# Banded attention scored per half block of queries, in plain fp32 on 32x64 tiles

## The chip, the cores and the metric

The kernel runs on one core of a Trainium2 chip. The metric is the device time of one execution in microseconds. The median of three runs of the kernel before is 2627.7 us (2626.91 to 2631.21).

## The reference, cut to what matters

8192 tokens of width 512 are layer-normalised; to the input are added a banded attention and a feed-forward. The attention has 16 heads of 32. Blocks are of 128 tokens, and a query sees the keys at a distance of at most 128:

```python
qkv = (xn @ Wqkv + bqkv).reshape(B, S, 3, H, Dh)
kwin = concat(previous block, own block, next block)      # 384 keys
scores = einsum('bhnqd,bhnkd->bhnqk', qb, kwin) / sqrt(512)
mask = (abs(kpos - qpos) <= 128) & (kpos >= 0) & (kpos < S)
attn = softmax(where(mask, scores, -1e30))
out = einsum('bhnqk,bhnkd->bhnqd', attn, vwin) ; out @ Wout + bout
x + attention(xn) + feed_forward(xn)
```

## The kernel before, in words

The program has three stages: it prepares the feed-forward's weights, runs the feed-forward over all tokens and leaves its result (`partial`) and the transposed, normalised tokens in DRAM, and then runs `attention_stage`, from about 1130 us to the end. Only this last stage is changed.

It goes over 32 tiles `i` of two blocks (256 tokens) and, in each, over 4 groups `c` of four heads: 128 steps `t`, `i, c = where(t)`. The order on every engine is written out by hand as a loop over `t`, with semaphores between the engines. The letters used below: `b` is one of the tile's two blocks, `h` one of the group's four heads, `u = 4b + h`.

On TensorE (PE) one step is, in this order:

- `scores(t, 0)` (L1176): for the four heads, each on its own 32-row tile of the array and in its own PSUM bank, 128 queries by 384 keys. Queries and keys are kept as a high and a low part in the fast reduced format (`q_hi`, `q_lo`, `k_hi`, `k_lo`, type F32R), so that three passes (high x high, low x high, high x low) make up one product: 12 matmuls.
- four turns of `turn_probs(t-1, 1, part)` (L1193), three 128x128 transposes of one head's probabilities by a matmul with the identity, and `run_a(t, part)` (L1105), six of the 24 matmuls that project queries and keys for step `t + 2`.
- `scores(t, 1)`.
- `probs_times_values(t-1)` (L1217): plain fp32, the four heads on four 32-column tiles of the array. Two key blocks are seen by both query blocks (256 columns), two by one of them (128 columns): 16 matmuls, all into one bank.
- four turns of `turn_probs(t, 0, part)` and `run_b(t, part)`: three of the 12 matmuls of a V projection (L1114) or of the output projection (L1123).

VectorE (DVE) finds each row's maximum with the mask added while it copies the scores out of PSUM (`find_max`, L1006), takes reciprocals (L1017), normalises three heads of four (L1021), and writes the low parts `q_lo`, `k_lo` (`qk_low`, L1034, L1038) and `oT_lo` (L1027). ScalarE (ACT) does the exponentials (`exp`, L928), copies the transposed probabilities out of PSUM (`copy_pT`, L938), and writes `q_hi`, `k_hi` (`qk_high`, L954, L957), `oT_hi` (L946) and the values (`take_v`, L921). GpSimd (POOL) normalises the fourth head (L888), copies the last two key blocks of a tile to the front of the ring in every second tile (`copy_keys`) and adds the output's bias. SyncE (SP) holds the DMA queue: tokens in, `partial` in, `out` out.

`values` is a ring of 6 blocks, `oT_hi` and `oT_lo` hold two tiles (8 slots). PE waits for a block of V by `v_done`.

Of the kernel before, what the change touches and what calls it, by code (L numbers as in the profile page):

```python
# [22 lines left out]
P = 128  # L23
# [638 lines left out]
def attention_stage(nc, loaded, xT_dram, partial, out):  # L662
# [6 lines left out]
    VR = 6  # L669
    XR = 3  # L670

    ctx = ExitStack()
    with ctx:
# [14 lines left out]
        mask = sb("mask", [P, 3 * P], F32)  # L688
# [13 lines left out]
        oT_hi = sb("oT_hi", [P, 2, DC, T], F32R)  # L702
        oT_lo = sb("oT_lo", [P, 2, DC, T], F32R)
# [13 lines left out]
        k0_hi, k0_done = sem("k0_hi"), sem("k0_done")  # L717
        qk_hi_done, qk_done = sem("qk_hi_done"), sem("qk_done")
        keys_copied = sem("keys_copied")
        v_done = sem("v_done")  # L720
        scored = sem("scored")
# [40 lines left out]
        def window(i, b):  # L762
            first, last = max(2 * i - 1 + b, 0), min(2 * i + 1 + b, NBLK - 1)
            base = 2 * i - 1 + b
            return slice((first - base) * P, (last - base + 1) * P)

        def blocks_seen(i, b):

            return range(0 if 2 * i - 1 + b >= 0 else 1, 3 if 2 * i + 1 + b < NBLK else 2)
# [22 lines left out]
        def job_release(n):  # L792

            t, k = divmod(n, 3)
            if k == 0:
                return (qk_done, job_a(t) + 1) if job_a(t) is not None else None
            if k == 1:
                return (oT_done, t) if 1 <= t <= STEPS else None
            b = job_b(t)
            if b is None:  # L800
                return None
            return (v_done, 2 * b[1] + b[2] + 2) if b[0] == "v" else (out_added, 2 * b[1] + b[2] + 1)

        def wait_job_bank(pe, n):
# [6 lines left out]
            elif n % 2 == 0:  # L811
                pe.wait_ge(v_done, 2)
            else:
                pe.wait_ge(qk_done, 2)
# [17 lines left out]
        def _(sp):  # L832
# [18 lines left out]

            for j in range(-1, XR - 1):
                load_x(j)
            sp.wait_ge(wout_lo_done, 1)
            for b in range(2):
                load_part(0, b)
            for i in range(NT + 1):
                if 1 <= i:
# [4 lines left out]
                if i + XR - 1 < NT:  # L863
                    load_x(i + XR - 1)
            for b in range(2):
# [3 lines left out]
        def _(pool):  # L869
            identity_on_pool(pool, nc, ident, zeroed, ident_done)  # L870
            nc.gpsimd.memset(mask[:, :], 0.0).then_inc(zeroed, 1)
            pool.wait_ge(zeroed, 2)
            nc.gpsimd.affine_select(out=mask[:, 0:P], in_=mask[:, 0:P], compare_op=ALU.is_ge, fill=NEG,
                                    base=0, pattern=[[1, P]], channel_multiplier=-1).then_inc(mask_done, 1)
            nc.gpsimd.affine_select(out=mask[:, 2 * P:3 * P], in_=mask[:, 2 * P:3 * P], compare_op=ALU.is_ge,
                                    fill=NEG, base=0, pattern=[[-1, P]], channel_multiplier=1).then_inc(mask_done, 1)
# [6 lines left out]
            def normalise_last_head(t, b):  # L883
                i, _ = where(t)
                cols = window(i, b)
                u = b * HC + HC - 1
                pool.wait_ge(rcp_done, 2 * (2 * t + b) + 2)
                nc.gpsimd.tensor_scalar(probs[:, u, cols], probs[:, u, cols], sum_rcp[:, u:u + 1], None, ALU.mult  # L888
                                        ).then_inc(last_head_normalised, 1)

            def copy_keys(u):
                i, c = where(u)
                pool.wait_ge(qk_done, u + 1)
                nc.gpsimd.tensor_copy(k_hi[:, c, 0:2, :], k_hi[:, c, 4:6, :])
                nc.gpsimd.tensor_copy(k_lo[:, c, 0:2, :], k_lo[:, c, 4:6, :]).then_inc(keys_copied, 1)
# [20 lines left out]
        def _(act):  # L916
            def take_v(i, r, number, bank):
                act.wait_ge(job_filled, number)
                if i >= 2:
                    act.wait_ge(pv_done, 4 * i - 4)  # L920
                nc.scalar.copy(values[:, (2 * i + 1 + r) % VR, :], job_ps[:, bank, :]).then_inc(v_done, 1)  # L921

            def exp(t, b, h):
                i, _ = where(t)
                cols = window(i, b)
                u = b * HC + h
                act.wait_ge(maxed, 8 * t + u + 1)
                nc.scalar.activation(probs[:, u, cols], probs[:, u, cols], ACT.Exp, bias=neg_max[:, u:u + 1], scale=-1.0,  # L928
                                     accum_out=prob_sum[:, u:u + 1]).then_inc(exped, 1)

            def copy_pT(t, b, h):
                i, _ = where(t)
                seen = blocks_seen(i, b)
                first = 3 * at(i, b)
# [3 lines left out]
                nc.scalar.copy(pT[:, h, first + seen.start:first + seen.stop, :].rearrange("p w t -> p (w t)"),  # L938
                               pT_ps[:, h % 2, seen.start * P:seen.stop * P]).then_inc(pT_done, 1)

            def oT_high(t):
                i, c = where(t)
                act.wait_ge(pv_done, t + 1)
                if i >= 2 and c == 0:
                    act.wait_ge(job_filled, B_NUMBER[4 * (i - 1) + 2])
                nc.scalar.copy(oT_hi[:, i % 2, c, :], job_ps[:, pv_bank(t), 0:T]).then_inc(oT_hi_done, 1)  # L946

            def qk_high(u, number, bank):
# [3 lines left out]
                if u >= DC:  # L952
                    act.wait_ge(scored, 2 * (u - DC) + 2)
                nc.scalar.activation(q_hi[:, c, :, :].rearrange("p b t -> p (b t)"), job_ps[:, bank, 0:T], ACT.Identity,  # L954
                                     bias=qk_bias[:, c:c + 1], scale=1.0)
                half = new_keys_at(i)
                nc.scalar.activation(k_hi[:, c, half:half + 2, :].rearrange("p b t -> p (b t)"),  # L957
                                     job_ps[:, bank, T:2 * T], ACT.Identity,
                                     bias=qk_bias[:, DC + c:DC + c + 1], scale=1.0).then_inc(qk_hi_done, 1)
# [393 lines left out]
```

## Time and profile before

| | us |
|---|---|
| median of the runs | 2627.7 |
| profiled execution, its own time | 2629.41 |
| its span, first to last instruction | 2627.6 |
| PE busy | 2576.2 (98%) |
| ACT busy | 1638.1 (62%) |
| DVE busy | 1592.0 (61%) |
| POOL busy | 631.8 (24%) |
| mean granted clock of PE | 0.989 |

PE's matmuls are pipelined, so a record's duration is longer than the time between two starts; what a matmul costs in a stream is read from the starts. PEld is the load of the stationary operand, which lies beside the matmul before. A plain fp32 matmul leaves two load records and two matmul records. In a form such as "128*32 128x256" the first pair is rows and columns of the stationary operand, the second the moving one.

### The profile page before, as it was taken

To read this page: it belongs to the slowest core of one execution; us is meant where nothing else is said; L and a number is where in the kernel's file an instruction comes from. 1 tells how busy PE (TensorE), PEld (TensorE's weight loads), DVE (VectorE), ACT (ScalarE), POOL (GpSimd) and SP (SyncE) were. 2 spreads that over 40 slices of the span, in tenths; PEclk is the share of its full clock that TensorE was granted. 3 is DMA by queue.
4 is the path that set the end of the run, shared out by engine and by line. 5 is a ranking of instruction groups with operands and counts; after the bars stand their busy time and mean duration, and the time that the engine had idled before them with its cause. 6 is when DMAs were issued, how large, how long until landed. Compare 5 with 4: busy or idle time off the path is not lost.

```text
span 2627.6 us, 55989 instructions
## 1 busy us (share of the span) xinstructions
PE 2576.2 (98%) x19728; PEld 2090.2 (80%) x19728; DVE 1592.0 (61%) x4779; ACT 1638.1 (62%) x4260; POOL 631.8 (24%) x595
## 2 busy tenths in 40 slices
PE   6999999999999999989999999999999999999998
PEld 4888888888888888868888888888888888888885
DVE  5444444444444444357777777777777777777775
ACT  6333333333333333358888888888888888888886
POOL 0011111111111111033333333333333333333332
PEclk7999999999999999999999999999999999999999
DMA  5422222222222222021121111112111111112110
GB/s 181 146 80 81 80 80 80 80 80 80 80 80 80 80 80 64 33 81 34 34 65 34 53 46 42 58 41 58 34 61 39 42 58 42 58 34 65 34 46 29
DMA packets 188361, 167.43 MB, mean 64 GB/s; under 512 B 11328, under 2 KB 143424, under 8 KB 187632
## 3 DMA queue, kind: packets, MB, share of 16 engines
q1 hardware_dynamic: 188000, 164.41, 20.2%
q8 instruction: 132, 2.16, 0.4%
q14 instruction: 85, 0.70, 0.1%
q0 software_dynamic: 144, 0.17, 0.0%
HBM read 97.43 MB, written 67.11 MB: 63 GB/s over the span
## 4 chain that ended last, share of the span: by engine, by line
PE 55%; ACT 1%; issue 0%; DVE 0%; POOL 0%; POOLq 0%; ACTq 0%
PE pT_ps L1193 14%; PE job_ps L1105 14%; PE score_ps L1176 7%; PE job_ps L1123 7%; PE job_ps L1217 7%; PE job_ps L1114 7%; ACT wqkv_raw L928 1%; ACT wqkv_raw L938 0%; PE job_ps L1237 0%; PE score_ps L1227 0%; DVE wqkv_raw L1006 0%; DVE k_lo L1038 0%; ACT q_hi L954 0%; ACT k_hi L957 0%; POOL wout_raw L899 0%
## 5 line engine op out<-in xcount | busy, mean ns | idle before, releaser
L928 ACT ACTIVATE wqkv_raw<-wqkv_raw,neg_max 128x384 f32<-128x384 f32 (+1 forms) x1024 | 633.3, 619 | 186.3 <-DVE neg_max L1006 181.5
L888 POOL TENSOR_SCALAR wqkv_raw<-wqkv_raw,sum_rcp 128x384 f32<-128x384 f32 (+1 forms) x256 | 372.9, 1457 | 960.1 <-DVE sum_rcp L1017 960.1
L494 ACT ACTIVATE relu<-up_ps,fc_scale 128x512 f32<-128x512 f32 x256 | 176.2, 688 | 656.2 <-PE up_ps L625 656.2
L938 ACT COPY wqkv_raw<-pT_ps 128x384 f32<-128x384 f32 (+1 forms) x1024 | 484.7, 474 | 74.4 <-PE pT_ps L1193 74.1
L1193 PE MATMUL pT_ps<-ident,wqkv_raw 128*128 128x128 f32 x3040 | 513.4, 277 | 8.1 <-ACT wqkv_raw L938 7.7
L1006 DVE CUSTOM_DVE_ANT_0 wqkv_raw<-score_ps,mask 128x384 f32<-128x384 f32 (+1 forms) x1024 | 503.5, 548 | 5.7 <-PE score_ps L1176 1.6
L568 DVE SCALAR_TENSOR_TENSOR sq<-up_ps,relu 128x512 f32<-128x512 f32 x256 | 177.0, 692 | 531.8 <-ACT relu L494 530.4
L1193 PEld LDWEIGHTS pT_ps<-ident,wqkv_raw 128*128 128x128 f32 x3040 | 360.0, 140 | 119.1 <-ACT wqkv_raw L938 42.6
L635 PE MATMUL down_ps<-proj_T,sq_hi 128*128 128x512 f32 x1024 | 408.9, 399 | 0.9 <-DVE sq_lo L551 0.9
L637 PE MATMUL down_ps<-proj_T,sq_lo 128*128 128x512 f32 x1024 | 404.3, 395 | 0.0
L621 PE MATMUL up_ps<-f_xT_hi,fc_T 128*128 128x512 f32 x1024 | 399.2, 390 | 1.4 <-DVE low L539 1.4
L623 PE MATMUL up_ps<-f_xT_lo,fc_T 128*128 128x512 f32 x1024 | 399.2, 390 | 0.0
L1105 PE MATMUL job_ps<-xT_hi,wqkv_hi 128*128 128x256 f32 x1024 | 329.0, 321 | 0.1
L1021 DVE TENSOR_SCALAR wqkv_raw<-wqkv_raw,sum_rcp 128x384 f32<-128x384 f32 (+1 forms) x768 | 298.2, 416 | 17.9
L1017 DVE RECIPROCAL sum_rcp<-prob_sum 128x2 f32<-128x2 f32 x512 | 85.0, 166 | 354.5 <-ACT wqkv_raw L928 354.0
L1105 PE MATMUL job_ps<-xT_hi,wqkv_lo 128*128 128x256 f32 x1024 | 287.9, 281 | 0.0
L1105 PE MATMUL job_ps<-xT_lo,wqkv_hi 128*128 128x256 f32 x1024 | 287.8, 281 | 0.0
L454 POOL TENSOR_TENSOR f_y<-f_y,part_in 128x512 f32<-128x512 f32 x64 | 86.9, 1389 | 665.1 <-DVE f_y L559 665.1
L635 PEld LDWEIGHTS down_ps<-proj_T,sq_hi 128*128 128x128 f32 x1024 | 193.4, 189 | 43.9 <-DVE sq_lo L551 2.2
L621 PEld LDWEIGHTS up_ps<-f_xT_hi,fc_T 128*128 128x128 f32 x1024 | 192.3, 188 | 44.0 <-DVE low L539 2.2
L637 PEld LDWEIGHTS down_ps<-proj_T,sq_lo 128*128 128x128 f32 x1024 | 193.0, 188 | 43.0
L623 PEld LDWEIGHTS up_ps<-f_xT_lo,fc_T 128*128 128x128 f32 x1024 | 192.3, 188 | 42.5
(126 smaller groups left out, 4228.2 us busy)
## 6 DMA issues: line engine op xcount, KB each, us to landing
xT_hi<-xT SPq DMA_DIRECT2D x65, 256.0 KB, 3.8
xT_lo<-xT SPq DMA_DIRECT2D x65, 256.0 KB, 4.5
f_x_in<-in_L_attn_x SPq DMA_DIRECT2D x64, 256.0 KB, 3.2
xT<-f_xT_hi SPq DMA_DIRECT2D x64, 256.0 KB, 2.6
xT<-f_xT_lo SPq DMA_DIRECT2D x64, 256.0 KB, 2.8
part_in<-in_L_attn_x SPq DMA_DIRECT2D x64, 256.0 KB, 3.4
partial<-f_y SPq DMA_DIRECT2D x64, 256.0 KB, 2.0
wout_raw<-partial SPq DMA_DIRECT2D x64, 256.0 KB, 2.8
```

Of the source, the lines that this page charges most:

```text
L621: nc.tensor.matmul(up_ps[:, s % 2, :], fc_T[:, k, cols], xT_hi[:, par, k, :], start=(k == 0), stop=False)
L623: nc.tensor.matmul(up_ps[:, s % 2, :], fc_T[:, k, cols], xT_lo[:, par, k, :], start=False, stop=False)
L635: nc.tensor.matmul(down_ps[:, b, :], sq_hi[:, s % 2, t], proj_T[:, s, :], start=(s == 0), stop=False)
L637: last = nc.tensor.matmul(down_ps[:, b, :], sq_lo[:, s % 2, t], proj_T[:, s, :], start=False, stop=(s == FB - 1))
L888: nc.gpsimd.tensor_scalar(probs[:, u, cols], probs[:, u, cols], sum_rcp[:, u:u + 1], None, ALU.mult).then_inc(last_head_normalised, 1)
L928: nc.scalar.activation(probs[:, u, cols], probs[:, u, cols], ACT.Exp, bias=neg_max[:, u:u + 1], scale=-1.0, accum_out=prob_sum[:, u:u + 1] ...
L938: nc.scalar.copy(pT[:, h, first + seen.start:first + seen.stop, :].rearrange("p w t -> p (w t)"), pT_ps[:, h % 2, seen.start * P:seen.stop ...
L1006: nc.vector.tensor_tensor_reduce(out=probs[:, u, cols], in0=score_ps[:, h, cols], in1=mask[:, cols], scale=-SCORE_SCALE, scalar=3e38, op0= ...
L1021: nc.vector.tensor_scalar(probs[:, u, cols], probs[:, u, cols], sum_rcp[:, u:u + 1], None, ALU.mult).then_inc(normalised, 1)
L1105: last = nc.tensor.matmul(job_ps[:, bank, is_k * T:(is_k + 1) * T], w[:, k, col:col + P], tokens, start=(m == 0), stop=(m == PASSES * DC - 1))
L1114: last = nc.tensor.matmul(job_ps[:, bank, :], a[:, k, x_slot(i) + r, :], w[:, k, 2 * D:3 * D], start=(n == 0), stop=(n == PASSES * DC - 1))
L1193: last = nc.tensor.transpose(pT_ps[:, h % 2, w * P:(w + 1) * P], probs[:, u, w * P:(w + 1) * P], ident[:, :])
```

## The change

Each block of 128 queries is treated as two halves `s` of 64. A half sees 64 queries by 320 keys instead of 384: `KEYS = 320`, and in column `j` of half `s` stands the key `64 s + j` of the old window.

- Scores: queries and keys are kept once, as plain F32 (`queries`, `keys`). Head `h` and half `s` go to the 32x64 tile at row `32 h` and column `64 s`: 8 plain fp32 matmuls of 320 columns instead of 12 of 384. The copies of low parts (`qk_low`) are gone; ACT writes the queries (`take_q`), DVE the keys (`take_k`).
- The mask has 320 columns; at the two ends of the sequence the keys that don't exist are filled by a memset and the maximum is taken for each half apart.
- Transposes: an even head is transposed from column 0 in two pieces, an odd head from column 64 in two pieces, and the 64 columns left over by an even head (256 to 319) and by the odd head after it (0 to 63), which lie side by side in `probs`, in one more: five for two heads instead of six.
- Values: since the two halves' windows begin 64 keys apart, and odd heads are cut 64 keys further on than even ones, V is kept twice, in `values` and, shifted by 64 tokens, in `half_on`. The second copy is made by two DMAs per block on SP (`move_values`), and PE waits for them by `v_moved`. For each half there is a part of 2 x 64 columns, two of 64, and two of 64 on 64x32 tiles (64 keys only; even heads in rows 0 to 63, odd heads in rows 64 to 127): 40 matmuls instead of 16.
- `values` has a ring of 5, `oT_hi` and `oT_lo` one of 6 slots.

```diff
-    VR = 6
+    VR = 5
     XR = 3
+    HALF = P // 2
+    KEYS = 2 * P + HALF
+    OR = 6
+    FAR = -NEG * SCORE_SCALE
...
-        q_hi = sb("q_hi", [P, DC, 2, P], F32R)
-        q_lo = sb("q_lo", [P, DC, 2, P], F32R)
-        k_hi = sb("k_hi", [P, DC, 6, P], F32R)
-        k_lo = sb("k_lo", [P, DC, 6, P], F32R)
+        queries = sb("queries", [P, DC, 2, P], F32)
+        keys = sb("keys", [P, DC, 6, P], F32)
         values = sb("values", [P, VR, D], F32)
-        probs = wqkv_raw[:, 0:2, :].rearrange("p a (u k) -> p (a u) k", k=3 * P)
+        half_on = sb("values_half_on", [P, VR, D], F32)
+        probs = wqkv_raw.rearrange("p a n -> p (a n)")[:, 0:2 * HC * KEYS].rearrange("p (u k) -> p u k", k=KEYS)
...
+            def move_values(m):
+
+                sp.wait_ge(v_done, m + 1)
+                if m >= VR:
+                    sp.wait_ge(pv_done, 4 * ((m - VR + 1) // 2) + 4)
+                sp.dma_start(half_on[HALF:P, (m - 1) % VR, :], values[0:HALF, m % VR, :]).then_inc(v_moved, 16)
+                sp.dma_start(half_on[0:HALF, m % VR, :], values[HALF:P, m % VR, :]).then_inc(v_moved, 16)
...
+                if 2 * i + 2 < NBLK:
+                    move_values(2 * i + 2)
...
+                if 2 * i + 3 < NBLK:
+                    move_values(2 * i + 3)
...
-                if i >= 2:
-                    act.wait_ge(pv_done, 4 * i - 4)
+                m = 2 * i + 1 + r
+                if m >= VR:
+                    act.wait_ge(pv_done, 4 * ((m - VR + 1) // 2) + 4)
+                    act.wait_ge(v_moved, 32 * (m - VR + 1))
...
-                if i >= 2 and c == 0:
-                    act.wait_ge(job_filled, B_NUMBER[4 * (i - 1) + 2])
-                nc.scalar.copy(oT_hi[:, i % 2, c, :], job_ps[:, pv_bank(t), 0:T]).then_inc(oT_hi_done, 1)
-
-            def qk_high(u, number, bank):
+                if i >= 1 and c == OR - DC:
+                    act.wait_ge(job_filled, B_NUMBER[4 * i + 2])
+                nc.scalar.copy(oT_hi[:, t % OR, :], job_ps[:, pv_bank(t), 0:T]).then_inc(oT_hi_done, 1)
...
-            def qk_low(u, bank):
+                nc.vector.tensor_tensor(oT_lo[:, t % OR, :], job_ps[:, pv_bank(t), 0:T],
+                                        oT_hi[:, t % OR, :].bitcast(F32), ALU.subtract).then_inc(oT_done, 1)
+
+            def take_k(u, bank):
                 i, c = where(u)
                 half = new_keys_at(i)
-                dve.wait_ge(qk_hi_done, u + 1)
-                nc.vector.scalar_tensor_tensor(q_lo[:, c, :, :].rearrange("p b t -> p (b t)"), job_ps[:, bank, 0:T],
-                                               qk_bias[:, c:c + 1],
-                                               q_hi[:, c, :, :].rearrange("p b t -> p (b t)").bitcast(F32),
-                                               ALU.add, ALU.subtract)
-                nc.vector.scalar_tensor_tensor(k_lo[:, c, half:half + 2, :].rearrange("p b t -> p (b t)"),
-                                               job_ps[:, bank, T:2 * T], qk_bias[:, DC + c:DC + c + 1],
-                                               k_hi[:, c, half:half + 2, :].rearrange("p b t -> p (b t)").bitcast(F32),
-                                               ALU.add, ALU.subtract).then_inc(qk_done, 1)
+                dve.wait_ge(q_done, u + 1)
+                nc.vector.tensor_scalar(keys[:, c, half:half + 2, :].rearrange("p b t -> p (b t)"),
+                                        job_ps[:, bank, T:2 * T], qk_bias[:, DC + c:DC + c + 1], None, ALU.add
+                                        ).then_inc(k_done, 1)
...
-                for pass_ in range(PASSES):
-                    q = q_lo if pass_ == 1 else q_hi
-                    keys = k_lo if pass_ == 2 else k_hi
-                    for h in range(HC):
-                        rows = slice(h * DH, (h + 1) * DH)
-                        last = nc.tensor.matmul(score_ps[:, h, cols], q[rows, c, place, :],
-                                                keys[rows, c, first + seen.start:first + seen.stop, :],
-                                                start=(pass_ == 0), stop=(pass_ == PASSES - 1),
-                                                tile_position=(h * DH, 0))
+                for h in range(HC):
+                    rows = slice(h * DH, (h + 1) * DH)
+                    window = keys[rows, c, :, :].rearrange("p a t -> p (a t)")
+                    for s in range(2):
+                        start = (keys_start(i) + b) * P + s * HALF
+                        first, last_ = first_key(i, b, s), last_key(i, b, s)
+                        last = nc.tensor.matmul(score_ps[half_rows(s), h, first:last_],
+                                                queries[rows, c, at(i, b), half_rows(s)],
+                                                window[:, start + first:start + last_],
+                                                start=True, stop=True, tile_position=(h * DH, s * HALF))
...
-                for w in blocks_seen(i, b):
-                    last = nc.tensor.transpose(pT_ps[:, h % 2, w * P:(w + 1) * P], probs[:, u, w * P:(w + 1) * P],
+                for w in range(2):
+                    start = w * P + h % 2 * HALF
+                    last = nc.tensor.transpose(pT_ps[:, h % 2, w * P:(w + 1) * P], probs[:, u, start:start + P],
                                                ident[:, :])
+                if h % 2:
+                    both = probs[:, u - 1:u + 1, :].rearrange("p u k -> p (u k)")[:, 2 * P:3 * P]
+                    last = nc.tensor.transpose(pT_ps[:, 1, 2 * P:3 * P], both, ident[:, :])
...
-                    pe.wait_ge(v_done, min(2 * i + 3, NBLK))
+                    pe.wait_ge(v_moved, 32 * min(2 * i + 3, NBLK))
                 pe.wait_ge(pT_done, 8 * t + 2 * HC)
-                parts = []
-                for blk in (2 * i, 2 * i + 1):
-                    first, second = (3 * place + blk - (2 * i - 1 + at(i, place)) for place in range(2))
-                    parts.append((blk, slice(0, 2), slice(first, second + 1, second - first)))
-                for b, blk in enumerate((2 * i - 1, 2 * i + 2)):
-                    if 0 <= blk < NBLK:
-                        place = at(i, b)
-                        seen = 3 * place + 2 * b
-                        parts.append((blk, slice(place, place + 1), slice(seen, seen + 1)))
-                for n, (blk, places, seen) in enumerate(parts):
-                    for h in range(HC):
-                        head = c * HC + h
-                        strip = slice(h * DH, (h + 1) * DH)
-                        last = nc.tensor.matmul(job_ps[strip, bank, places.start * P:places.stop * P],
-                                                values[:, blk % VR, head * DH:(head + 1) * DH], pT[:, h, seen, :],
-                                                start=(n == 0), stop=(n == len(parts) - 1), tile_position=(0, h * DH))
+                for s in range(2):
+                    for part in range(5):
+                        for h in range(HC):
+                            head = c * HC + h
+                            strip = slice(h * DH, (h + 1) * DH)
+                            odd = h % 2
+                            v = half_on if s != odd else values
+                            base = 2 * i - 1 + (s if odd else 0)
+                            rows, row = slice(0, P), 0
+                            if part == 0:
+                                blk, places = base + 1, slice(0, 2)
+                                first, second = (3 * place + 1 - at(i, place) for place in range(2))
+                                seen = slice(first, second + 1, second - first)
+                            elif part < 3:
+                                b = part - 1
+                                blk, place = base + 2 * b, at(i, b)
+                                places, seen = slice(place, place + 1), slice(3 * place + b, 3 * place + b + 1)
+                                if blk < 0 and not odd and s == 0:
+                                    continue
+                            else:
+                                b = part - 3 if odd else 4 - part
+                                if 2 * i + b == (0 if odd else NBLK - 1):
+                                    continue
+                                place, rows, row = at(i, b), half_rows(odd), odd * HALF
+                                blk = base + b + (-1 if odd else 2)
+                                places, seen = slice(place, place + 1), slice(3 * place + 2, 3 * place + 3)
+                            out_ = job_ps[strip, bank, 0:T].rearrange("p (a t) -> p a t", t=P)[:, places, half_rows(s)]
+                            last = nc.tensor.matmul(out_, v[rows, blk % VR, head * DH:(head + 1) * DH],
+                                                    pT[rows, h | 1 if part > 2 else h, seen, half_rows(s)],
+                                                    start=(part == 0), stop=(part == 4), tile_position=(row, h * DH))
```

On PE, from the last scores of a step over the values to the first transposes, where the tile's newest block of V is waited for (`score_ps` scores, `job_ps<-wqkv_raw` probabilities times values, `pT_ps` transposes), before:

```order
L1176 MATMUL score_ps<-k_hi,q_hi 128x384 [waits maxed]
L1176 MATMUL score_ps<-k_hi,q_hi 128x384 x3
L1176 MATMUL score_ps<-k_hi,q_lo 128x384 x4
L1176 MATMUL score_ps<-k_lo,q_hi 128x384 x4
L1217 MATMUL job_ps<-wqkv_raw,values 32x256 [waits pT_done,v_done]
L1217 MATMUL job_ps<-wqkv_raw,values 32x256 x7
L1217 MATMUL job_ps<-wqkv_raw,values 32x128 x8
L1193 MATMUL pT_ps<-ident,wqkv_raw 128x128 [waits normalised,pT_done]
```

and with the change (line numbers of the changed kernel):

```order
L1191 MATMUL score_ps<-keys,queries 64x320 [waits maxed]
L1191 MATMUL score_ps<-keys,queries 64x320 x7
L1249 MATMUL job_ps<-wqkv_raw,values 32x2x64 [waits pT_done,v_moved,v_done]
L1249 MATMUL job_ps<-wqkv_raw,values_half_on 32x2x64
L1249 MATMUL job_ps<-wqkv_raw,values 32x2x64
L1249 MATMUL job_ps<-wqkv_raw,values_half_on 32x2x64
L1249 MATMUL job_ps<-wqkv_raw,values 32x64
L1249 MATMUL job_ps<-wqkv_raw,values_half_on 32x64
```

Sixteen matmuls of 64 columns follow the four of 2 x 64, by turns on `values` and `half_on`, the last eight of them on 64x32 tiles; then the same 20 once more for the other half. The order around them has not moved.

On PE, the start of a step after the first scores, before, a head's transposes ahead of six projections:

```order
L1193 MATMUL pT_ps<-ident,wqkv_raw 128x128 [waits normalised,pT_done]
L1193 MATMUL pT_ps<-ident,wqkv_raw 128x128 x2
L1105 MATMUL job_ps<-xT_hi,wqkv_hi 128x256
L1105 MATMUL job_ps<-xT_lo,wqkv_hi 128x256
L1105 MATMUL job_ps<-xT_hi,wqkv_lo 128x256
```

and with the change, two heads:

```order
L1208 MATMUL pT_ps<-ident,wqkv_raw 128x128 [waits normalised,pT_done]
L1208 MATMUL pT_ps<-ident,wqkv_raw 128x128
L1123 MATMUL job_ps<-xT_hi,wqkv_hi 128x256 [waits oT_done]
L1123 MATMUL job_ps<-xT_lo,wqkv_hi 128x256
L1123 MATMUL job_ps<-xT_hi,wqkv_lo 128x256
L1123 MATMUL job_ps<-xT_hi,wqkv_hi 128x256
L1123 MATMUL job_ps<-xT_lo,wqkv_hi 128x256
L1123 MATMUL job_ps<-xT_hi,wqkv_lo 128x256
L1208 MATMUL pT_ps<-ident,wqkv_raw 128x128 [waits normalised,pT_done]
L1208 MATMUL pT_ps<-ident,wqkv_raw 128x128
L1212 MATMUL pT_ps<-ident,wqkv_raw 128x128
```

An even head has two transposes, an odd one three.

On SP's queue, one tile in the steady part, with the change:

```order
L866 DMA values_half_on<-values 64x512 [waits pv_done,v_done]
L867 DMA values_half_on<-values 64x512
L859 DMA out<-wout_raw 128x512 [waits y_done]
L855 DMA wout_raw<-partial 128x512 [waits out_added]
L859 DMA out<-wout_raw 128x512 [waits y_done]
L855 DMA wout_raw<-partial 128x512 [waits out_added]
L849 DMA xT_hi<-xT 128x4x128 [waits job_filled]
L849 DMA xT_hi<-xT 128x4x128
L849 DMA xT_lo<-xT 128x4x128 x2
L866 DMA values_half_on<-values 64x512 [waits pv_done,v_done]
```

The moves (L866, L867) are new, ahead of the two stores and behind the loads of tokens; the rest stands as before.

## Rows read from the trace of the kernel before

**Rows 1.** The page, busy us, share of the span and instructions of each engine.
```profile
PE 2576.2 (98%) x19728; PEld 2090.2 (80%) x19728; DVE 1592.0 (61%) x4779; ACT 1638.1 (62%) x4260; POOL 631.8 (24%) x595
```
**Rows 2.** Stretch of the steady steps: us, busy (x) by engine, PEclk, DMA share, GB/s.
```profile
1378.37:2522.73 1144.36, 1144.36 (x11601) 933.04 (x11600) 837.68 (x2950) 941.09 (x2752) 391.78 (x350) 1.00 0.16 48
```
**Rows 3.** Waits, 1500 to 2500 us: who <- whom: us, times, longest.
```profile
POOL wqkv_raw L888 <- DVE sum_rcp L1017: 657.7, 175, 4.6
DVE sum_rcp L1017 <- ACT wqkv_raw L928: 243.4, 350, 1.1
ACT wqkv_raw L928 <- DVE neg_max L1006: 124.7, 88, 1.4
...
PEld score_ps L1176 <- issue: 32.0, 88, 0.4
```
**Rows 4.** Chain, 1801.7 to 1813.3 us: start, us up to the next piece, what.
```profile
1801.84 0.73 PE score_ps L1176 x9
1802.57 0.48 PE pT_ps L1193 x3
1803.05 0.71 PE job_ps L1105 x6
1803.76 0.33 PE pT_ps L1193 x3
...
1807.59 1.44 PE job_ps L1217 x32
...
1809.51 0.70 PE job_ps L1123 x3
```
**Rows 5.** Timeline of PE, narrow windows in one values part: first start, us, matmuls overlapping.
```profile
1807.53 0.42 PE L1217 MATMUL job_ps<-wqkv_raw,values 128*32 128x256 f32 x4
1807.77 0.61 PE L1217 MATMUL job_ps<-wqkv_raw,values 128*32 128x256 f32 x8
1808.20 0.51 PE L1217 MATMUL job_ps<-wqkv_raw,values 128*32 128x256 f32 x8
1808.41 0.51 PE L1217 MATMUL job_ps<-wqkv_raw,values 128*32 128x128 f32 x12
1808.63 0.40 PE L1217 MATMUL job_ps<-wqkv_raw,values 128*32 128x128 f32 x8
1808.96 0.55 PE L1193 MATMUL pT_ps<-ident,wqkv_raw 128*128 128x128 f32 x3
```
**Rows 6.** Line L1217, 1807.5 to 1808.3: ns min/median/max, first and last start.
```profile
L1217 PE MATMUL job_ps<-wqkv_raw,values x16: 379/379/404, 1807.5 to 1808.2; 128*32 128x256 f32 x16
```
**Rows 7.** Timeline of PE, 1806.7 to 1807.4 us, the three score passes.
```profile
1806.80 0.45 PE L1176 MATMUL score_ps<-k_hi,q_hi 32*128 32x384 f32 x4
1807.09 0.34 PE L1176 MATMUL score_ps<-k_hi,q_lo 32*128 32x384 f32 x4
1807.26 0.34 PE L1176 MATMUL score_ps<-k_lo,q_hi 32*128 32x384 f32 x4
```
**Rows 8.** ACT's timeline, and line L1217 on PE: V's copy and its reader.
```profile
1435.95 0.61 ACT L921 COPY values<-job_ps 128x512 f32<-128x512 f32 x1
...
L1217 PE MATMUL job_ps<-wqkv_raw,values x32: 272/326/404, 1441.3 to 1442.6; 128*32 128x256 f32 x16, 128*32 128x128 f32 x16
```
**Rows 9.** The page, DMA issues on SP: KB each, median us to landing.
```profile
xT_lo<-xT SPq DMA_DIRECT2D x65, 256.0 KB, 4.5
...
partial<-f_y SPq DMA_DIRECT2D x64, 256.0 KB, 2.0
```
**Rows 10.** Chain while the pipeline fills, 1130 to 1170 us.
```profile
1158.42 0.37 ACT k_hi L957
1158.81 0.48 DVE q_lo L1034
```
**Rows 11.** The tail: its chain, and its stretch (columns as in rows 2).
```profile
2611.45 2.40 PE job_ps L1217 x24
...
2600.00:2628.00 28.00, 17.83 (x120) 11.58 (x112) 8.55 (x31) 9.09 (x30) 6.67 (x6) 0.80 0.11 39
```

More of the change, by code:

```diff
@@ L760, in new_keys_at, with half_rows, first_key, last_key @@
             return keys_start(i) + 2
[L762 to L769, printed above, removed]
+        def half_rows(s):
+            return slice(s * HALF, (s + 1) * HALF)
+        def first_key(i, b, s):
+            return max(0, -((2 * i - 1 + b) * P + s * HALF))
+        def last_key(i, b, s):
+            return min(KEYS, (NBLK - (2 * i - 1 + b)) * P - s * HALF)
+        def at_edge(i, b):
+            return 2 * i + b == 0 or 2 * i + b == NBLK - 1
         def job_a(t):
@@ L937, in copy_pT @@
                     act.wait_ge(pv_done, t)
-                nc.scalar.copy(pT[:, h, first + seen.start:first + seen.stop, :].rearrange("p w t -> p (w t)"),
-                               pT_ps[:, h % 2, seen.start * P:seen.stop * P]).then_inc(pT_done, 1)
+                nc.scalar.copy(pT[:, h, first:first + count, :].rearrange("p w t -> p (w t)"),
+                               pT_ps[:, h % 2, 0:count * P]).then_inc(pT_done, 1)
             def oT_high(t):
@@ L953, in qk_high @@
                     act.wait_ge(scored, 2 * (u - DC) + 2)
[L954 to L959, printed above, removed]
+                nc.scalar.activation(queries[:, c, :, :].rearrange("p b t -> p (b t)"), job_ps[:, bank, 0:T],
+                                     ACT.Identity, bias=qk_bias[:, c:c + 1], scale=1.0).then_inc(q_done, 1)
             act.wait_ge(wqkv_here, 64)
@@ L1005, in find_max @@
                     u = b * HC + h
[L1006 to L1008 removed]
+                    if not at_edge(i, b):
+                        nc.vector.tensor_tensor_reduce(out=probs[:, u, :], in0=score_ps[:, h, 0:KEYS], in1=mask[:, :],
+                                                       scale=-SCORE_SCALE, scalar=3e38, op0=ALU.add, op1=ALU.min,
+                                                       accum_out=neg_max[:, u:u + 1]).then_inc(maxed, 1)
+                        continue
+                    for s in range(2):
+                        rows, first, last = half_rows(s), first_key(i, b, s), last_key(i, b, s)
+                        outside = slice(0, first) if first else slice(last, KEYS)
+                        nc.vector.memset(probs[rows, u, outside], FAR)
+                        done = nc.vector.tensor_tensor_reduce(out=probs[rows, u, first:last],
+                                                              in0=score_ps[rows, h, first:last], in1=mask[rows, first:last],
+                                                              scale=-SCORE_SCALE, scalar=3e38, op0=ALU.add, op1=ALU.min,
+                                                              accum_out=neg_max[rows, u:u + 1])
+                    done.then_inc(maxed, 1)
             def normalise(t, b):
[L1011 to L1012 removed]
                 for pair in range(2):
@@ L1059, in _ @@
             nc.vector.tensor_tensor(out_bias[:, :], score_ps[:, 0, :], bout_wide[:, :], ALU.add).then_inc(bias_added, 1)
-            dve.wait_ge(mask_done, 2)
-            dve.wait_ge(k0_hi, 1)
-            for c in range(DC):
-                last = nc.vector.scalar_tensor_tensor(k_lo[:, c, keys_start(0) + 1, :], job_ps[:, 0, c * P:(c + 1) * P],
-                                                      qk_bias[:, DC + c:DC + c + 1],
-                                                      k_hi[:, c, keys_start(0) + 1, :].bitcast(F32), ALU.add, ALU.subtract)
-            last.then_inc(k0_done, 1)
+            dve.wait_ge(mask_done, 4)
             for u in range(2):
-                qk_low(u, u)
+                take_k(u, u)
             for t in range(STEPS + 3):
@@ L1122, in project_out @@
                     a = oT_lo if o_low else oT_hi
-                    last = nc.tensor.matmul(job_ps[:, bank, :], a[:, i % 2, k, at(i, b) * P:(at(i, b) + 1) * P],
+                    last = nc.tensor.matmul(job_ps[:, bank, :], a[:, (DC * i + k) % OR, at(i, b) * P:(at(i, b) + 1) * P],
                                             w[:, k, :], start=(n == 0), stop=(n == PASSES * DC - 1))
```

80 lines of the change are left out of this document (37 added, 43 removed).

## The prediction

> **What bounds the kernel now.** I read the page's shares first, then the stretches, the waits, the chain and last the single matmul starts. PE is busy 98% of the span [rows 1]. The change touches only the attention stage, the last 1,500 us. Its steady part is the stretch from 1378.37 to 2522.73 us, 100 steps (11,601 matmul records, 116 to a step). PE is busy in all of the 1144.36 us, ACT 941 (82%), DVE 838 (73%), POOL 392 (34%), at clock 1.00, the 2.4 GHz level [rows 2]. One step is therefore 11.44 us of PE, and no other engine fills it. The waits agree: in 1,000 us POOL waits for DVE, DVE for ACT and ACT for DVE; for PE's matmuls there is no line at all, and its weight loads have lines of at most 32 us, once a step, which lie beside a matmul that still runs [rows 3]. The chain gives the step piece by piece, each up to the next piece's start [rows 4]: scores 0.73, twice; transposes three at a time, 0.33, or 0.48 right after scores or values; six projections 0.71; values 1.44; three output (or V) projections 0.70. With four turns each for the two projections that adds up to 11.5. So only PE's time counts, and each piece must be repriced.
>
> **Prices from single starts.** In the values part four matmuls, one per 32-column tile, start together. Groups of 256 columns start 0.215 us apart (1807.77 to 1808.20 is two groups), groups of 128 columns 0.11 [rows 5]. Each plain fp32 matmul leaves two records, so 256 columns cost 2 x 0.215: time goes with columns. Four groups of each make 1.30 of the 1.44; 0.14 is left. It splits as follows: the last group (0.11 after 1808.63, so 1808.74) is followed by the transposes at 1808.96, 0.22 instead of 0.11, so 0.11 for changing the tiling; and the longest of them took 404 ns where the median is 379, 0.025 for a weight load that nothing covers [rows 6]. In the scores a pass of four matmuls of 384 columns costs 0.17, the first one 0.29 [rows 7]; 0.73 less three passes leaves 0.22 for entering, leaving and an uncovered load of 128 columns.
>
> **The change part by part, per step.**
> Transposes: 20 instead of 24, each 0.33/3 = 0.11 [rows 4]: **-0.44**. In the runs of two after a change of tiling the extra 0.15 (0.48 against 0.33) stays.
> Scores: 8 plain fp32 matmuls of 320 columns in 8 tiles replace 12 of 384 in 4 tiles. If all 8 run side by side, two records of 0.215 x 320/256 = 0.27 take the place of three passes of 0.17: 0.54 for 0.51. Around them 0.22 stays, or 0.17 if the uncovered load of 64 columns is half of that of 128 (0.29 - 0.17 = 0.12). That is +0.03 or -0.02 each, two a step: between +0.06 and -0.04. I take **0**, from the middle, since the load is smaller but twice as many matmuls must start.
> Values: 40 matmuls for 16. Each query half has one part of 2 x 64 columns and four of 64, two records each: together 4 groups of 128 columns and 16 of 64. The first are 4 x 0.11 = 0.44. The second are not in the trace; by columns they are 0.055 each, 0.88. Together 1.32 for 1.30: +0.02. Columns streamed are the same; the parts are only cut finer.
> Changes of tiling inside the values: the last two parts of each half have 64 rows, so the tiles go 128x32, 64x32, 128x32, 64x32: three changes where none was. No row shows a change of the row height alone. Lower bound 0 (the columns of the tiles stay), upper bound 0.22 (all that surrounds the scores). The nearest row is the exit from the values themselves, 0.11 and 0.025 for the load: I take 0.14. Three of them: **+0.42**, between 0 and +0.66.
> Sum: -0.44 + 0 + 0.02 + 0.42 = **0.00 us a step**.
>
> **Off PE, costed at nothing.** Subtracting and writing q_lo and k_lo goes, k is written once by DVE; every exp, maximum and normalisation has 320 columns, every second copy of transposes 256. All this relieves ACT, DVE and POOL, which have 200 us and more of cover in the steady part [rows 2]; if PE became faster by 0.4 us a step they would still not be reached. At the two ends of the sequence the maximum is split in two and a fill is added, in 8 of 128 steps, under the same cover. The ring for the output's operands shrinks from 8 slots to 6: ACT's copy at every fourth step now waits for an output projection that PE ends half a step earlier. Nothing queues behind it.
> New is the move of V: two DMAs of 128 KB per block on SP's queue, and PE's first values matmul of each four steps waits for them. The copy of V ends at 1435.95 + 0.61 = 1436.56 and PE starts on that block at 1441.3 [rows 8], so 4.7 us of cover. No row shows a copy within SBUF; transfers of twice its size on the same queue land after 2.0 to 4.5 us [rows 9]. SP reaches the move in time: what stands ahead waits for events of the step before, and the stores queued behind it wait for output projections that come later. Price 0; if the slower end and the second DMA's place in the queue add up to 5.7 us, 1 us x 32 blocks = 32 us.
> Outside the steady part the other engines are on the path. While the pipeline fills, the chain holds k_hi and q_lo, 0.37 + 0.48 [rows 10], and the same two a second time later; both go: -0.85 x 2. In the tail some ten exps and copies on the chain lose a sixth of about 0.5 us, -0.8, against three more changes of tiling in the last values, which take 2.40 at a mean clock of 0.80 in that stretch [rows 11]: +0.4. Together -2.
>
> So the profiled execution, 2629.4, becomes 2627.4. The median of the runs lies 1.7 below it, which gives **2625 us**, no change: 0.2% of 2627.7 is 5.3 us, what a measurement of this kernel can tell. It is 0.04 us a step, less than my prices are good for: the forecast's own spread of +-0.12 a step is 2610 to 2640.
>
> **Rivals.**
> A, the change of tiling is nearly free, since the column tiles stay and only the row height changes. Then 0.42 falls away: -54, **2571**. For it: the values keep their four 32-column tiles throughout. Against: the exit from the values costs its 0.11 and the surroundings of the scores 0.22, so no change of tiling in the trace is free.
> B, on the other side: **groups of 64 columns do not get below 0.11**, because four loads and four starts per group need it. In the trace the densest stretch is four matmuls per 0.11 us, 27 ns each [rows 5]; the change asks for 14 ns each. 16 groups x 0.055 = +0.88 a step, +113, **2738**; from 0.059 us per group on the change is slower by over 0.2%. Against it: the first four matmuls span 0.42 us together where the longest takes 0.404, so they start within 20 ns [rows 5, 6], and the time of a group halves exactly with its columns from 256 to 128, as a stream does and a start does not. The Trainium skill (TensorE: Matmul & The Clock Gate, section "Wait — 56ns, not 53.3ns?") has a floor of about 25 ns from start to start however small the matmul; by it a group costs 0.10 and the time would be about 2717. The trace neither reaches below it in the mean (27 ns) nor keeps to it inside a group.
> C, the 64-row parts take turns: even heads sit in rows 0 to 63, odd ones in rows 64 to 127, and both write one PSUM bank. That doubles 8 groups of 0.055: +0.44, +56, **2681**. The Trainium skill (TensorEngine Tiling (Array Packing), section "Gotcha 1: PSUM Pressure") says that different row tiles cannot access the same bank at the same time. In the trace the four row tiles of the scores each have their own bank and the four column tiles of the values share one, so neither speaks for or against; their output partitions differ, as those of the column tiles do.
> D, the change does not do what it says: the two column halves of a row tile take turns in the scores, which then cost 4 x 0.27. +0.54 x 2 = 1.08 a step, +138, **2763**. The trace has four row tiles side by side and four column tiles side by side, not both at once.
> E, V's move is late: +32, about 2657.
>
> **How the numbers follow.** Forecast 50% (18 faster, 17 same, 15 slower), A 16, B and its milder forms, groups between 0.06 and 0.11, 13, C 9, D 7, E and others 5. Faster 0.18 + 0.16 + 0.01 = 0.35; same 0.18; slower 0.47. The range takes in A and, upwards, C, E and B with groups of up to 0.10 (16 x 0.045 x 128 = 92 us): 2570 to 2720. It leaves out D and the full B, about 14%.
>
> **What would show it.** Right: in steady state a period of 11.44 us; transposes 0.22 and 0.33 by turns; scores near 0.73, with two groups of eight starts 0.27 apart; values near 1.9 us with gaps of 0.2 at three places; no PE wait for V's move. A shows as values of 1.5; B as small groups 0.11 apart; C as parts three and four alone at 0.11; D as scores of 1.3; E as PE idle before the values of every fourth step. A period off by more than 0.12 us makes the forecast wrong.

## The result, and the profile after

The changed kernel takes 2646.36 us (median of 4 runs, 2645.09 to 2647.46), the kernel before beside it 2629.45. The ratio is 1.0065, with an interval from 1.0047 to 1.0082: slower by 0.65%, where no change was forecast. Run once more beside the experiments it gave 2647.11 us and a ratio of 1.0068 (1.0054 to 1.0081). The profiled execution has a span of 2645.7 us against 2627.6, 18.1 us more.

The steady steps came out as priced. The chain of waits of the changed kernel in one of them (start, us up to the next piece, what), which answers to [rows 4]:

```profile
1813.41 0.72 PE score_ps L1191 x16
1814.14 1.87 PE job_ps L1249 x80
1816.01 0.37 PE pT_ps L1208 x2
1816.38 0.70 PE job_ps L1141 x3
1817.08 0.22 PE pT_ps L1208 x2
1817.30 0.11 PE pT_ps L1212
```

The scores take 0.72 us, as before (0.73). The values take 1.87 instead of 1.44. The transposes take 0.22 and 0.33 by turns, 0.37 right after a change of tiling. The stretch that answers to [rows 2] is again filled by PE, while the other engines are relieved (columns as there):

```profile
1378.37:2522.73 1144.36, 1144.36 (x16795) 901.59 (x16780) 733.88 (x2850) 871.07 (x2649) 337.02 (x299) 1.00 0.21 60
```

16,795 matmul records at 168 a step are 100 steps in 1144.36 us, as before. Read from the first scores of steps 4 and 124, the period is 11.453 us against 11.442. Over the steady part that is 1.3 us, so 17 of the 18 lie elsewhere. The first scores of single steps, read from PE's timeline, show where:

| us | before | changed | difference |
|---|---|---|---|
| first scores of step 0 | 1154.0 | 1155.7 | +1.7 |
| step 0 to step 4 | 41.4 | 45.8 | +4.4 |
| step 4 to step 124 | 1373.1 | 1374.4 | +1.3 |
| step 124 to the end | 59.1 | 69.8 | +10.7 |

The pipeline fills in steps 0 to 3 and drains in steps 124 to 127, and these are the steps with the blocks at the edge of the sequence. There the changed kernel's DVE does this for one head (timeline: start us, us; line 1034 is the fill, 1035 the maximum):

```profile
1157.63 0.17 DVE L1034 MEMSET wqkv_raw<- 64x128 f32 x1
1157.81 0.35 DVE L1035 CUSTOM_DVE_ANT_0 wqkv_raw<-score_ps,mask 64x192 f32<-64x192 f32 x1
1158.09 0.08 DVE L1035 DVE_READ_ACCUMULATOR2_ANT neg_max<- 64x1 f32 x1
1158.22 0.11 DVE L1034 MEMSET wqkv_raw<- 64x64 f32 x1
1158.34 0.43 DVE L1035 CUSTOM_DVE_ANT_0 wqkv_raw<-score_ps,mask 64x256 f32<-64x256 f32 x1
1158.70 0.08 DVE L1035 DVE_READ_ACCUMULATOR2_ANT neg_max<- 64x1 f32 x1
1158.86 0.17 DVE L1034 MEMSET wqkv_raw<- 64x128 f32 x1
```

and the kernel before at the same place:

```profile
1155.06 0.42 DVE L1006 CUSTOM_DVE_ANT_0 wqkv_raw<-score_ps,mask 128x256 f32<-128x256 f32 x1
1155.40 0.08 DVE L1006 DVE_READ_ACCUMULATOR2_ANT neg_max<- 128x1 f32 x1
1155.40 0.42 DVE L1006 CUSTOM_DVE_ANT_0 wqkv_raw<-score_ps,mask 128x256 f32<-128x256 f32 x1
```

From one head to the next it is 1.23 us (1157.63 to 1158.86) where it was 0.34 (1155.06 to 1155.40). The two halves don't cost half each: a maximum of 64 rows by 256 columns takes 0.43 us, one of 128 rows by 256 took 0.42. So an instruction was doubled, and a fill added to each; the two fills are 0.28 of the 1.23 us. No experiment parts the fills from the doubling. 32 heads (four heads, four steps, two ends) by 0.89 are 28 us of DVE work.

It is on the path. The chain of the changed kernel in its drain:

```profile
2595.77 0.11 DVE wqkv_raw L1034
2595.90 0.42 DVE wqkv_raw L1035
2596.32 0.07 issue
2596.39 0.17 DVE wqkv_raw L1034
2596.57 0.36 DVE wqkv_raw L1035
```

and its waits, 2576 to 2646 us (who <- whom: us in total, times, longest):

```profile
ACT wqkv_raw L954 <- DVE neg_max L1035: 8.2, 10, 1.7
```

PE's granted clock is lower too: its mean is 0.83 from 2576 to 2646 us, against 0.91 in the drain before. From 2580 to 2587.4 us PE was busy in 5.4 of 7.4 us, at a clock of 1.00; from 2587.92 to 2589.85 the clock is 0.50, which is the 1.2 GHz level. This piece of the drain's chain lies there; the same six projections take 0.71 in a steady step:

```profile
2587.92 0.65 PE pT_ps L1208 x2
2588.57 1.28 PE job_ps L1123 x6
```

Theory T, then: the loss is due to the split maxima at the two ends, on DVE, in the 8 steps in which PE does not cover them. Rival R: the ends lose because exponentials, normalisations, copies and values are no longer cut there to the 256 keys that exist. And for the steady part the prediction's 0.14 us for a change of tiling stands against rival S: the changes are cheap, and the finer parts make the 0.43.

### The profile page after: what moved, and what is told of

Read it like the earlier page. It is cut to its first block, busy times and chain, and to the rows that moved or that the text cites. A ratio compares the mean times of both kernels' runs of the same rounds, so it can differ in the third digit from the quotient of the medians.

```text
span 2645.7 us, 69331 instructions
## 1 busy us (share of the span) xinstructions
PE 2589.0 (98%) x26400; PEld 2061.6 (78%) x26400; DVE 1482.3 (56%) x4775; ACT 1555.6 (59%) x4132; POOL 567.9 (21%) x534
## 4 chain that ended last, share of the span: by engine, by line
PE 54%; DVE 1%; ACT 1%; issue 0%; POOLq 0%; POOL 0%; ACTq 0%; DVEq 0%
PE job_ps L1123 13%; PE pT_ps L1208 10%; PE job_ps L1249 9%; PE job_ps L1132 7%; PE score_ps L1191 7%; PE job_ps L1141 7%; PE pT_ps L1212 2%; DVE wqkv_raw L1035 1%; ACT wqkv_raw L954 0%; DVE wqkv_raw L1034 0%; PE job_ps L1269 0%; PE score_ps L1259 0%; ACT wqkv_raw L963 0%; DVE wqkv_raw L1050 0%; DVE keys L1063 0%
## 5 line engine op out<-in xcount | busy, mean ns | idle before, releaser
L954 ACT ACTIVATE wqkv_raw<-wqkv_raw,neg_max 128x320 f32<-128x320 f32 x1024 | 579.1, 566 | 152.4 <-DVE neg_max L1027 136.6
L915 POOL TENSOR_SCALAR wqkv_raw<-wqkv_raw,sum_rcp 128x320 f32<-128x320 f32 x256 | 326.7, 1276 | 1043.4 <-DVE sum_rcp L1046 1043.4
L963 ACT COPY wqkv_raw<-pT_ps 128x256 f32<-128x256 f32 (+1 forms) x1024 | 434.4, 424 | 167.9 <-PE pT_ps L1208 113.3
L1027 DVE CUSTOM_DVE_ANT_0 wqkv_raw<-score_ps,mask 128x320 f32<-128x320 f32 x992 | 426.3, 486 | 65.4 <-PE score_ps L1191 59.2
L1208 PE MATMUL pT_ps<-ident,wqkv_raw 128*128 128x128 f32 x2048 | 405.9, 280 | 7.8 <-ACT wqkv_raw L963 7.5
L1208 PEld LDWEIGHTS pT_ps<-ident,wqkv_raw 128*128 128x128 f32 x2048 | 251.6, 140 | 136.8 <-issue 60.7
L1050 DVE TENSOR_SCALAR wqkv_raw<-wqkv_raw,sum_rcp 128x320 f32<-128x320 f32 x768 | 273.8, 385 | 18.0
L1249 PE MATMUL job_ps<-wqkv_raw,values 64*32 64x64 f32 (+2 forms) x5072 | 250.4, 235 | 2.0 <-ACT wqkv_raw L963 2.0
L1249 PEld LDWEIGHTS job_ps<-wqkv_raw,values 64*32 64x32 f32 (+1 forms) x5072 | 190.0, 109 | 76.3 <-issue 64.8
L1249 PE MATMUL job_ps<-wqkv_raw,values_half_on 64*32 64x64 f32 (+2 forms) x5088 | 248.9, 235 | 0.0
```

The lines of the kernel that those rows point to most:

```text
L915: nc.gpsimd.tensor_scalar(probs[:, u, :], probs[:, u, :], sum_rcp[:, u:u + 1], None, ALU.mult).then_inc(last_head_normalised, 1)
L954: nc.scalar.activation(probs[:, u, :], probs[:, u, :], ACT.Exp, bias=neg_max[:, u:u + 1], scale=-1.0, accum_out=prob_sum[:, u:u + 1]).then ...
L963: nc.scalar.copy(pT[:, h, first:first + count, :].rearrange("p w t -> p (w t)"), pT_ps[:, h % 2, 0:count * P]).then_inc(pT_done, 1)
L1027: nc.vector.tensor_tensor_reduce(out=probs[:, u, :], in0=score_ps[:, h, 0:KEYS], in1=mask[:, :], scale=-SCORE_SCALE, scalar=3e38, op0=ALU. ...
L1050: nc.vector.tensor_scalar(probs[:, u, :], probs[:, u, :], sum_rcp[:, u:u + 1], None, ALU.mult).then_inc(normalised, 1)
L1208: last = nc.tensor.transpose(pT_ps[:, h % 2, w * P:(w + 1) * P], probs[:, u, start:start + P], ident[:, :])
```

## The experiments

**e1: the maximum at the ends in one instruction.** The changed kernel, where the two end blocks use masks of their own that also exclude the keys that don't exist; the scores are computed over all 320 columns there, over a key block set to zero at the start and over a stale one at the end.

```diff
-        mask = sb("mask", [P, KEYS], F32)
+        mask = sb("mask", [P, 3, KEYS], F32)
...
+                nc.gpsimd.memset(mask[rows, 1, 0:first_key(0, 0, s)], NEG).then_inc(mask_done, 1)
+                nc.gpsimd.memset(mask[rows, 2, last_key(NT - 1, 1, s):KEYS], NEG).then_inc(mask_done, 1)
...
-                    for s in range(2):
-                        rows, first, last = half_rows(s), first_key(i, b, s), last_key(i, b, s)
-                        outside = slice(0, first) if first else slice(last, KEYS)
-                        nc.vector.memset(probs[rows, u, outside], FAR)
-                        done = nc.vector.tensor_tensor_reduce(...)
+                    kind = (1 if i == 0 else 2) if at_edge(i, b) else 0
+                    nc.vector.tensor_tensor_reduce(out=probs[:, u, :], ..., in1=mask[:, kind, :], ...)
...
-                        first, last_ = first_key(i, b, s), last_key(i, b, s)
+                        first, last_ = 0, KEYS
```

> Of the changed kernel, with one thing undone: the two end blocks of the sequence take their maximum in one instruction per head, against a mask of their own, instead of two half-row instructions and two fills. Theory T (the 17 us lost lie in the filling and draining of the pipeline, where the split maxima on DVE, 1.23 us a head instead of 0.41, are on the path for 8 steps): 26 us of DVE work go, most of the loss with them, so 2629 to 2634 us, the end steps 125 to 127 as in the kernel before to within 2 us; steady period unchanged at 11.45. Rival R (the ends lose because exponentials, copies and values there are no longer cut to 256 keys): 2642 to 2646.

Measured: 2631.67 us (11 runs), ratio 1.0012 to the kernel before (1.0003 to 1.0021). 14.7 us of the 16.9 are back by the medians; against the kernel before, run beside each, +16.9 has become +3.6, which is 13.3 us. DVE goes from head to head in 0.41 us (timeline):

```profile
1156.24 0.08 DVE L1036 DVE_READ_ACCUMULATOR2_ANT neg_max<- 128x1 f32 x1
1156.24 0.49 DVE L1036 CUSTOM_DVE_ANT_0 wqkv_raw<-score_ps,mask 128x320 f32<-128x320 f32 x1
1156.65 0.09 DVE L1036 DVE_READ_ACCUMULATOR2_ANT neg_max<- 128x1 f32 x1
1156.65 0.49 DVE L1036 CUSTOM_DVE_ANT_0 wqkv_raw<-score_ps,mask 128x320 f32<-128x320 f32 x1
```

Step 0 to step 4 takes 39.6 us and step 124 to the end 57.1, the period is still 11.453. T holds and R falls: the exponentials, copies and normalisations at the ends have the full 320 columns here too, and the scores now as well. In the last steps the chain runs over ACT and no longer over the maxima:

```profile
2602.71 0.66 ACT wqkv_raw L963 x2
2603.37 0.26 ACT wqkv_raw L972
2603.64 0.55 ACT wqkv_raw L963 x2
```

In the two profiles part of the difference is the clock's. The values of step 125 in the drain take 3.23 us in the changed kernel, at a mean clock of 0.50, and 1.92 in e1, at 1.00 (chains of the changed kernel and of e1):

```profile
2605.08 3.23 PE job_ps L1249 x72
```

```profile
2594.43 1.92 PE job_ps L1248 x72
```

How much of the loss is waiting for DVE and how much the lower clock is not separated. The profile of e1 is also that of its fastest run, 2627.76 us, 3.9 below its median.

**e3: the split put into the kernel before.** Nothing else is changed; the fills write columns that nobody reads.

```diff
...
+                    for s in range(2):
+                        rows = slice(s * P // 2, (s + 1) * P // 2)
+                        spare = 0 if cols.start else 2 * P
+                        nc.vector.memset(probs[rows, u, spare:spare + (s + 1) * P // 2], 0.0)
+                        done = nc.vector.tensor_tensor_reduce(out=probs[rows, u, cols], in0=score_ps[rows, h, cols], ...)
...
```

> Of the kernel before, with the split maximum of the change at the two end blocks added (two half-row instructions and two fills per head, nothing else changed). Theory T: about 0.8 us a head more on DVE, 32 heads, most of it on the path: +12 to +22 us over the kernel before, all outside the steady steps. Rival R: less than +4 us.

Measured: 2648.09 us, ratio 1.0075 (1.0061 to 1.0089), +20.0 us. Step 0 to step 4 takes 48.9 us for 41.4, step 124 to the end 69.3 for 59.1, and the period stays at 11.441. The split alone brings a loss of this size, in the same places. A half here has 256 columns where the change has 192 in one of two:

```profile
1156.56 0.11 DVE L1014 MEMSET wqkv_raw<- 64x64 f32 x1
1156.69 0.42 DVE L1015 CUSTOM_DVE_ANT_0 wqkv_raw<-score_ps,mask 64x256 f32<-64x256 f32 x1
1157.18 0.17 DVE L1014 MEMSET wqkv_raw<- 64x128 f32 x1
1157.36 0.43 DVE L1015 CUSTOM_DVE_ANT_0 wqkv_raw<-score_ps,mask 64x256 f32<-64x256 f32 x1
1157.86 0.11 DVE L1014 MEMSET wqkv_raw<- 64x64 f32 x1
```

1.30 us a head (1156.56 to 1157.86), which is the dearer of the two versions.

**e2: one change of tiling inside the values.** The same 40 matmuls in another order. The two halves' sums are now open at the same time in one bank, and they are started and stopped together: `start` stands at the first half's first part alone, `stop` at the second half's last.

```diff
-                for s in range(2):
-                    for part in range(5):
+                for s, part in ((0, 0), (1, 0), (0, 1), (0, 2), (1, 1), (1, 2), (0, 3), (0, 4), (1, 3), (1, 4)):
...
-                                                    start=(part == 0), stop=(part == 4), ...
+                                                    start=(part == 0 and s == 0), stop=(part == 4 and s == 1), ...
```

> Of the changed kernel, with the ten groups of the values in another order: first all parts on 128x32 tiles for both halves, then all on 64x32 tiles, so one change of tiling inside the values instead of three. If a change costs the 0.14 us that I took (0.11 and 0.025 uncovered load), the values take 1.60 instead of 1.87, the period 11.18 instead of 11.45, and the time falls by 2 x 0.14 x 128 = 35 us to about 2611. Rival S (the changes cost little, and the finer parts are what makes the values 1.87): the period stays above 11.40, time above 2640. The ends of the pipeline are as in the changed kernel under either.

Measured: 2612.03 us, ratio 0.9934 to the kernel before (0.9920 to 0.9947), 34.3 us below the changed kernel. The period is 11.187 us. In the chain, the values:

```profile
1820.13 0.72 PE score_ps L1191 x16
1820.85 1.60 PE job_ps L1249 x80
```

**e5: eight changes of tiling.** The same 40 matmuls again, with parts on the two tilings taking turns.

```diff
-                for s in range(2):
-                    for part in range(5):
+                for s, part in ((0, 0), (0, 3), (0, 1), (0, 4), (0, 2), (1, 0), (1, 3), (1, 1), (1, 4), (1, 2)):
...
-                                                    start=(part == 0), stop=(part == 4), ...
+                                                    start=(part == 0), stop=(part == 2), ...
```

> Of the changed kernel, with the parts of the values ordered so that parts on 128x32 and on 64x32 tiles take turns: eight changes of tiling inside the values instead of three, same matmuls. At 0.14 us each: +0.70 us a step, values 2.57, period 12.15, time +89 us, about 2735. Rival S (changes cost little): +0 to +20 us.

Measured: 2731.35 us, ratio 1.0388 (1.0371 to 1.0405), 85 us above the changed kernel. The values in its chain:

```profile
1816.31 0.72 PE score_ps L1191 x16
1817.04 2.56 PE job_ps L1249 x80
```

With 1, 3 and 8 changes the values take 1.60, 1.87 and 2.56 us: 0.135 and 0.138 a change, on one line. From the medians it is (2646.36 - 2612.03)/(2 x 128) = 0.134 and (2731.35 - 2646.36)/(5 x 128) = 0.133. S falls.

**e4: both edits together.**

> The changed kernel with both edits: end blocks' maxima in one instruction against masks of their own, and one change of tiling inside the values. The two lie in different stretches, so their gains (14.7 us and 34.3 us) should add: 2597 us, 1.2% below the kernel before. If the drain were bound by PE after the first edit or the steady steps by another engine after the second, the sum would fall short: above 2602.

Measured: 2598.5 us, ratio 0.9882 to the kernel before (0.9867 to 0.9898), period 11.187, step 124 to the end 57.2 us. The gains add to within 1.5 us. The time is 1.2% below the kernel before and 1.8% below the changed one.

**e6: the changed kernel again.**

> The changed kernel once more, unchanged, beside the others on one chip: 2646 us, 0.65% above the kernel before, period 11.45.

Measured: 2647.11 us, as told above. Its fill (48.55 us) and drain (67.05) are divided otherwise than in the first profile (45.8 and 69.8); the sum is 115.6 us in both, so the split between the two ends is not to be read to the microsecond. The clock is divided otherwise as well: its mean in the fill is 0.93 here and was 1.00, in the drain 0.86 and 0.83.

## Why the prediction was right and wrong

The kernel lost 17 us where no change was forecast. The steady steps, on which nearly all of the sum was spent, came out right; a term beside them that was put at nothing did not.

**What bounds the steady steps**, right: PE alone, at an 11.45 us period, with ACT at 871 of 1144 us and DVE at 734.

**The terms of the step**, right, all four. Transposes: 0.22 and 0.33 a turn, as priced. Scores: taken as 0 change, measured 0.72 for 0.73; all sixteen records of a block's scores lie in one stretch of that length, where D wanted 1.3, so the 8 tiles do run side by side and rival D falls. Values: +0.44 taken, +0.43 measured. Changes of tiling: 0.14 taken, 0.134 measured by e2 and e5, although only the height of the tiles changes; rival A falls. The sum of 0.00 a step came out as +0.01. (The last step of the forecast's own sum is rounded off: 2627.4 less 1.7 is 2625.7, not 2625.)

**Rivals B and C** fall by the timeline of the changed kernel: here is one record of each group of four (one on each column tile), first four groups on 128x32 tiles and then four on 64x32:

```profile
1814.31 0.22 PE L1249 MATMUL job_ps<-wqkv_raw,values 128*32 128x64 f32 x1
1814.37 0.22 PE L1249 MATMUL job_ps<-wqkv_raw,values 128*32 128x64 f32 x1
1814.42 0.22 PE L1249 MATMUL job_ps<-wqkv_raw,values 128*32 128x64 f32 x1
1814.48 0.22 PE L1249 MATMUL job_ps<-wqkv_raw,values 128*32 128x64 f32 x1
...
1814.65 0.24 PE L1249 MATMUL job_ps<-wqkv_raw,values 64*32 64x64 f32 x1
1814.73 0.22 PE L1249 MATMUL job_ps<-wqkv_raw,values 64*32 64x64 f32 x1
1814.78 0.22 PE L1249 MATMUL job_ps<-wqkv_raw,values 64*32 64x64 f32 x1
1814.84 0.22 PE L1249 MATMUL job_ps<-wqkv_raw,values 64*32 64x64 f32 x1
```

A group of four records follows the other every 0.056 us, 14 ns a record in the mean, in both tilings (1814.73 to 1814.84 is two groups); a matmul of the program leaves two records. The change of tiling stands between 1814.48 and 1814.65, 0.17 instead of 0.056, and the group after it takes 0.08. The floor of 25 ns that the Trainium skill (TensorE: Matmul & The Clock Gate, section "Wait — 56ns, not 53.3ns?") gives does not hold here, where the records go in turn to four column tiles. The Trainium skill (TensorEngine Tiling (Array Packing), section "Gotcha 1: PSUM Pressure") says that different row tiles cannot access the same bank at the same time. That did not decide here: the two row tiles write one bank, but different output partitions, and they do not take turns.

**Rival E** falls, and that 2646 lies near its 2657 is chance. The move of V lands 2.3 us after its issue by the list of DMAs from 1800 to 1900 us, and among PE's waits none is for it:

```profile
values_half_on<-values SPq DMA_DIRECT2D x8, 128.0 KB, 2.3
```

**Costed at nothing**, wrong, and this is the step that failed: "At the two ends of the sequence the maximum is split in two and a fill is added, in 8 of 128 steps, under the same cover." The cover, 200 us and more, is that of the steady part, from step 20 to step 120. The 8 steps are the first four and the last four of the stage, and the prediction itself says a little further down that outside the steady part the other engines are on the path. The 28 us of DVE work were never multiplied out. e1 puts the cost at 14.7 us, e3, with the dearer version, at 20.0. The sign that was to make the forecast wrong, a period off by more than 0.12 us, looks at the steady part alone and could not show this. Instead of the forecast gain of 2 us outside the steady part there was a loss of 17. Whether the gain is there without the split maxima is not shown: with e1 the fill is 1.8 us and the drain 2.0 us shorter than before in the profiles, but that profile is of its fastest run, with a mean clock of 0.99 in the drain where the one before has 0.91. The medians leave e1 at +3.6 us, of which 1.3 is the period. What makes up the other 2 us or more was not found. Nor was the 1.7 us before the first scores followed up; over all eight profiles these begin between 1154.0 and 1157.8 us.

## What to carry to other kernels

A cover is read from the stretch in which the work runs. Work at the ends of a sequence runs while a pipeline fills and drains, where the steady state's slack cannot be counted on: here 28 us of work cost about 15. Special cases for edges lie on the path there, and are better folded into data (a mask) than into more instructions. When many small matmuls use tiles of different shape, all of one shape should stand together: here the order alone was worth 34 us.

## What the runs showed of the hardware that I had not expected

- The maximum on 64 partitions costs DVE what it costs on 128: 0.43 us for 64x256 against 0.42 for 128x256. Split by rows it takes twice the time.
- Changing only the row height of the tiles (128x32 to 64x32 and back) costs PE 0.134 us each time, as much as leaving the values' tiling altogether cost before (0.11, and 0.025 for an uncovered load).
- Records of plain fp32 matmuls of 64 columns on four column tiles follow each other every 14 ns in the mean, in time proportional to their columns (0.056 us for a group of four, 0.11 with 128 columns); in the trace before the densest was 27.
- Eight 32x64 tiles run a plain fp32 product of 320 columns in the 0.72 us that three reduced passes of 384 columns on four tiles took.
